# The first of a tile's six down units done in three split products instead of one float32 product

## What is computed

```python
x = x + conv_ref(ln_c(x))            # a mixer over 7 x 7 windows, then an MLP
t = to_tokens(x)
t = t + ffn_ref(ln_t(t))             # a gated feed-forward, 2 of 4 experts
# the part of conv_ref that the change touches (C = 96, HID = 384):
y = ln(xr, ln2_w, ln2_b)
y = gelu(y @ W1 + b1) @ W2 + b2
return xr + y
```

## Time and profile before

| | before |
|---|---|
| median of 3 runs | 1864.97 us (1864.04 to 1866.19) |
| the profiled execution | 1863.09 us, of which the profile's span is 1861.4 us |
| PE busy | 1809.9 us, 97% |
| DVE busy | 1527.7 us, 82% |
| ACT busy | 1489.4 us, 80% |
| POOL busy | 1432.4 us, 77% |

### The profile page before, as it was taken

The page is one execution under the profiler, slowest core; times in us unless marked ns, Lnnn a source line. Parts: engine busy times, 40 slices in busy tenths (PEclk is TensorE's granted clock), DMA queues, the critical chain, the costliest instruction groups (busy, mean ns, idle before and its releaser), DMA issues.

```text
span 1861.4 us, 35592 instructions
## 1 busy us (share of the span) xinstructions
PE 1809.9 (97%) x8486; PEld 1258.2 (68%) x8486; DVE 1527.7 (82%) x6498; ACT 1489.4 (80%) x2823; POOL 1432.4 (77%) x1097
## 2 busy tenths in 40 slices
PE   5999999999999999999998999999999999999997
PEld 3566665666656666556776777777777777777775
DVE  6899999999999999987886777777777777777775
ACT  1677777777777777778997999999999999999996
POOL 3388888888888888876886878887777777777776
PEclk9999999999999999999998999999999999999999
DMA  6253443344443334335667766666666666666662
GB/s 192 84 166 121 129 125 122 110 122 126 125 125 113 121 121 127 108 124 156 203 208 233 218 214 210 212 213 204 210 210 209 209 205 205 205 205 212 214 209 82
DMA packets 139737, 312.03 MB, mean 168 GB/s; under 512 B 35066, under 2 KB 43925, under 8 KB 139530
## 3 DMA queue, kind: packets, MB, share of 16 engines
q1 hardware_dynamic: 104424, 249.10, 44.5%
q0 software_dynamic: 32000, 58.87, 9.0%
q10 hardware_dynamic: 3106, 1.78, 0.5%
HBM read 243.43 MB, written 67.19 MB: 167 GB/s over the span
## 4 chain that ended last, share of the span: by engine, by line
PE 53%; POOL 23%; issue 13%; DVE 7%; ACT 0%; DVEq 0%; POOLq 0%; ACTq 0%
POOL sorted_rows L522 12%; PE mix_ps L1298 8%; PE mix_ps L1300 8%; PE mix_ps L1299 8%; POOL rstd_xt L511 6%; PE turn_ps L1284 4%; PE up_ps L1284 4%; POOL rstd_r L498 4%; PE turn_ps L1285 4%; PE up_ps L1285 4%; PE turn_ps L1286 4%; PE up_ps L1286 4%; PE tok_ps L1309 4%; PE y_ps L1221 2%; DVE rows L857 1%
## 5 line engine op out<-in xcount | busy, mean ns | idle before, releaser
L570 POOL DMA_INDIRECT out<-out_sb,idx x412 | 430.3, 1045 | 240.8 <-DVE out_sb L1077 127.3
L1036 DVE TENSOR_TENSOR g_lo<-g,g_hi 128x512 fp32r<-128x512 f32 x618 | 423.9, 687 | 194.8 <-ACT g_hi L698 194.4
L522 POOL DMA_INDIRECT sorted_rows<-rows,pos x392 | 452.3, 1154 | 116.7 <-issue 102.4
L698 ACT CAST g_hi<-g 128x512 fp32r<-128x512 f32 x618 | 381.5, 617 | 13.1
L546 POOL TENSOR_TENSOR ex<-euler,rows 128x16 f32<-128x16 f32 x103 | 306.3, 2974 | 0.4
L1173 PE MATMUL y_ps<-g,d_mlp 128*100 128x512 f32 x588 | 292.7, 592 | 0.2 <-ACT g L630 0.2
L1298 PE MATMUL mix_ps<-g_hi,ew 128*96 128x512 f32 x618 | 244.7, 396 | 0.2 <-DVE g_lo L1036 0.2
L1300 PE MATMUL mix_ps<-g_lo,ew 128*96 128x512 f32 x618 | 244.5, 396 | 0.0
L1299 PE MATMUL mix_ps<-g_hi,ew 128*96 128x512 f32 x618 | 243.6, 394 | 0.0
L630 ACT ACTIVATE g<-up_ps 128x512 f32<-128x512 f32 x294 | 170.7, 597 | 64.6 <-PE up_ps L1166 54.6
L692 ACT ACTIVATE g<-up_ps 128x512 f32<-128x512 f32 x308 | 183.7, 597 | 39.8 <-PE up_ps L1286 26.9
(11 more groups left out here) (185 smaller groups left out, 3964.5 us busy)
## 6 DMA issues: line engine op xcount, KB each, us to landing
ew<-expert_w SPq DMA_DIRECT2D x206, 384.0 KB, 4.1
ew<-expert_w SPq DMA_DIRECT2D x206, 288.5 KB, 3.6
rows<-sorted_rows SPq DMA_DIRECT2D x103, 394.0 KB
x_in<-in_x SPq DMA_DIRECT2D x49, 384.0 KB, 3.1
x_raw_t<-in_x_chan SPq DMA_DIRECT2D x49, 384.0 KB, 4.9
rstd_t<-rstd_rows SPq DMA_DIRECT2D x49, 384.0 KB, 4.0
out<-out_sb,idx POOLq DMA_INDIRECT x412
sorted_rows<-rows,pos POOLq DMA_INDIRECT x392
```

The lines of the kernel that those rows point to most:

```text
L522: pool.indirect_dma_start(out=sorted_rows[:, :], out_offset=bass.IndirectOffsetOnAxis(ap=pos[:, r, s:s + 1], axis=0), in_=rows[:, r, s, :] ...
L570: pool.indirect_dma_start(out=out_rows, out_offset=bass.IndirectOffsetOnAxis(ap=idx[:, r, s:s + 1], axis=0), in_=out_sb[:, r, s, :], in_of ...
L698: act.copy(g_hi[:, n % PART_RING, :], g[:, n % G_RING, :]).then_inc(hi_done, 1)
L1036: dve.tensor_tensor(g_lo[:, n % PART_RING, :], g[:, n % G_RING, :], f(g_hi[:, n % PART_RING, :]), ALU.subtract).then_inc(lo_done, 1)
```

## The change

Unit 0 of each tile (the first of six, in period p for tile p) is no longer multiplied in one float32 product. Its values are split: ScalarE casts the high part (`first_hi`, between `gelu` 0 and `gelu` 1) and VectorE subtracts it for the low part (`first_lo`, between `positions` and the statistics of the mixer output). TensorE then makes three products of the parts with `d0_hi` and `d0_lo`, the parts of the unit's weights, which VectorE makes once at the start. The other five units stay as they are.

```diff
+        d0_hi = sb("d0_hi", [P, CG], F32R)
+        d0_lo = sb("d0_lo", [P, CG], F32R)
...
+            def first_hi(t):
+                act.wait_ge(gelu_done, UNITS * t + 1)
+                if t >= 1:
+                    act.wait_ge(down_done, UNITS * (t - 1) + 1)
+                act.copy(g_hi[:, PART_RING - 1, :], g[:, UNITS * t % G_RING, :]).then_inc(first_hi_ok, 1)
...
                 if tile(p):
                     gelu(p, 0)
+                    first_hi(p)
                     gelu(p, 1)
...
+                dve.wait_ge(gate_sums, GATE_SUMS)
+                dve.tensor_copy(d0_hi[:, :], d_mlp[:, 0, :]).then_inc(first_down_parts, 1)
+                dve.wait_ge(first_down_parts, 1)
+                dve.tensor_tensor(d0_lo[:, :], d_mlp[:, 0, :], f(d0_hi[:, :]), ALU.subtract).then_inc(first_down_parts, 1)
...
+            def first_lo(t):
+                dve.wait_ge(first_hi_ok, t + 1)
+                dve.tensor_tensor(g_lo[:, PART_RING - 1, :], g[:, UNITS * t % G_RING, :], f(g_hi[:, PART_RING - 1, :]),
+                                  ALU.subtract).then_inc(first_lo_ok, 1)
...
                 if p == KNOWN + 2:
                     dve.wait_ge(base_set, KNOWN + 1)
                     list_blocks(0, 0)
+                if tile(p):
+                    first_lo(p)
                 if tile(r):
                     dve.wait_ge(xr_summed, r + 1)
...
                 if k == 0 and m >= 1:
                     pe.wait_ge(y_copied, m)
+                if u == 0:
+                    pe.wait_ge(first_down_parts, 2)
+                    pe.wait_ge(first_lo_ok, t + 1)
+                    pe.matmul(y_ps[0:CG, :], d0_hi[:, :], g_hi[:, PART_RING - 1, :], start=True, stop=False)
+                    pe.matmul(y_ps[0:CG, :], d0_lo[:, :], g_hi[:, PART_RING - 1, :], start=False, stop=False)
+                    pe.matmul(y_ps[0:CG, :], d0_hi[:, :], g_lo[:, PART_RING - 1, :], start=False, stop=False).then_inc(down_done, 1)
+                    return
```

More of the change, by code:

```diff
@@ L258, in build_program @@
         h_summed, xr_summed, xr_turned = (sem(n) for n in ("h_summed", "xr_summed", "xr_turned"))
+        first_down_parts, first_hi_ok, first_lo_ok = sem("first_down_parts"), sem("first_hi_ok"), sem("first_lo_ok")
         up_done, down_done, y_turned = sem("up_done"), sem("down_done"), sem("y_turned")
```

## The result

| | before | after |
|---|---|---|
| median | 1865.49 us (1864.04 to 1866.81, 5 runs) | 2011.17 us (2010.47 to 2012.46, 5 runs) |
| span of the profiled execution | 1861.4 us | 2008.9 us |
| mean granted TensorE clock over the span | 0.995 | 0.962 |

The changed kernel is slower: the ratio is 1.0782, 95% interval 1.0769 to 1.0796. That is 145.7 us more, where the prediction had 89.9 and its range ended at 1970.

The account below looks back on a forecast made before the run. TensorE, streaming without a gap, bounds the kernel; a new wait for VectorE's low part closes a loop of 18.51 us a tile against 16.56. Over all tiles 89.9 us more: 1864.97 + 89.9 = 1954.9 us, range 1938 to 1970.

Parts of the forecast that it names:

- What bounds, and the wait: TensorE streams at 16.56 us a tile; VectorE, only 0.5 us late, makes down 0 wait for the low part.
- The loop's length: Down 0 through `to_channels`, `y_hi`, `y_lo` and `first_lo` back to down 0: 18.51 us a tile, 1.95 more.
- The hand-over from VectorE's subtraction to the product: From the end of `first_lo` to TensorE's first split product: 0.15 us, bounds 0.05 and 0.25.
- TensorE's gain: Down 0 as three split products takes 0.70 us instead of 0.86 in float32, saving 0.155 us a tile.
- ScalarE's cast: `first_hi` between gelu 0 and 1 charged nothing; without cover from TensorE's wait, up to 1.0 us a tile.
- VectorE's own loop: VectorE's work per tile plus the subtraction, 16.56 + 0.69 = 17.25 us; as rival "VectorE alone grows" 1897 us, 6%.
- First and last tiles and the sum: Tile 4 late by 6.3 us, tiles 5 to 44 add 78.0, tile 45 3.6, tiles 46 to 48 2: 89.9.
- The clock falls: Rival, 4%: TensorE's 2 us gap per tile lowers its clock for 5 us, 2.5 us each in 45 tiles, 2067 us.
- The gap is far nearer to the first: TensorE's 2 us gap resembles a 1.79 us idle stretch that kept 2.4 GHz, not the 5.83 us one at 1.2.

Follow-up runs that it names:

- filled kernel: Changed kernel plus seven throwaway TensorE products per tile ahead of the wait for the low part; 1954.12 us, ratio 1.0482 to the kernel before.

## Why the prediction was wrong, point by point

- **What bounds, and the wait.** Right. TensorE streams before; VectorE can be moved up by half a microsecond and no more; the wait for the low part closes a loop through `to_channels`, `y_hi` and `y_lo`.
- **The loop's length.** 18.51 predicted, 18.44 in tiles with the full clock. The gap was put at 2.08 and is 1.89 to 1.91. `y_lo` waits as said, but 0.6 us and not some 1; in a tile with the full clock VectorE stands another 0.61 us ahead of `add_x2`, for `turn_y`. The hand-over from VectorE's subtraction to the product, taken as 0.15, is 402.24 - 402.09 = 0.15. The rest is small: `y_hi` to `y_lo` takes 0.03 instead of 0.05, `y_lo` to `first_lo` 7.17 (414.28 to 421.45) for 7.16, and down 0 to the end of `to_channels` 9.20 (422.28 to 431.48) for 9.26.
- **TensorE's gain.** 0.155 us a tile, measured 0.16.
- **ScalarE's cast.** Nothing predicted; measured ratio 1.0002 (0.9992 to 1.0011). The bound of 1.0 us a tile without cover was too careful.
- **VectorE's own loop**, used for a rival only: 17.25 predicted, 16.96 measured. The duration of 0.69 stood for a step of 0.60, and the wait for GpSimd was taken as fixed, but 0.2 us of it was slack.
- **First and last tiles and the sum.** 89.9 predicted; with the gap filled the kernel takes 89.6 us more than before. The forecast of 1954.9 us is the time of that kernel, 1954.1, with a filled gap, which had no part in it. That it is so near is in part luck, since the terms err both ways. In the filled kernel down 0 is 8.8 us later than before in tile 4 (predicted 6.3), and 81.5 in tile 44, so the 40 tiles add 72.7 (predicted 78.0); tile 45 adds 3.5 (3.6), and what is behind it 4.7 (2).
- **The step that failed** is in the rival *The clock falls*: "The gap is far nearer to the first", with 4%. It set one idle stretch of 1.79 us, after which the clock stayed up, against one of 5.83, after which it was down, and took the nearer. Two errors are in it. One stretch is one case, and at the same gap the clock falls in some tiles and not in others: at 1.89 us 9 of 40 tiles would have read like that row. And the gap comes in some 45 tiles, and whether it brings the clock down goes by where the tile lies in the order of the falls, so a chance for the whole kernel was the wrong form for it; it should have been a share of tiles, and with both ends of that share in the range. So the sum charged the clock nothing, where the runs show 57 us (2011.17 against 1954.12 with the gap filled). The price of the rival was also mis-sized, in the other direction: 2.5 us a tile in 45 tiles, 2067 us, where it is 1.61 in 34.

The Trainium skill (TensorE: Matmul & The Clock Gate, Part 1) says that what watches TensorE's activity runs free of the kernel, so that the point at which the clock changes varies with where the work lands. The runs agree: a gap that is the same in every tile brings the clock down in some tiles and not in others, 31, 29 or 9 of 40 by its length, and the place of the fall moves on from tile to tile (0.40, 0.85, 1.27 us behind down 0). What the prediction took from that page, that a gap as in rows 9 keeps the clock up, the measurements don't bear out: gaps of 1.33 to 1.89 us brought it down. The rule of the Trainium skill (TensorE: Matmul & The Clock Gate, Step-by-step: what each phase is for) that matmuls stay in program order was borne out: up 2 needs nothing from down 0, and in the timelines it stands behind it, 403.00 after 402.24.

## What to carry to other kernels

When a change gives a streaming TensorE a wait that comes once in each round of a loop, sum the loop as usual, and then charge the clock for each round by itself: a gap that left the clock up once may bring it down in most rounds. Where such a gap has to stay, products that feed nothing are a cheap cure and a sharp test; here seven of them a tile, 1.6 us of work, took 57 us off the changed kernel. They cure the clock alone: the 90 us of the loop stay. And before an operand for TensorE is put on another engine, look at where in that engine's order it would be made against where TensorE needs it: an engine with 18% of idle time still had only half a microsecond to give at that place.

None of the versions beats the kernel before. VectorE's 0.60 us a tile outweigh the 0.16 that TensorE gains, even where no wait of TensorE is in the way.

## What the runs showed of the hardware that I had not expected

Behind a gap of 1.89 us TensorE runs at its full clock for a while, 0.3 to 1.6 us in the steady tiles, and only then falls to 1.2 GHz, for 3.41 us, while it is busy without a break. A gap of 1.33 us did so in 9 of 40 tiles, one of 1.18 us in 1 of 40, one of 0.86 us in none. The tiles that fall come in a regular order, at 1.33 us each fourth, from tile 10 on. What exactly is counted, idle time alone or also the short products of `sum_xr` ahead of the gap, these runs don't tell apart: in all of them the gap ends at the start of down 0, and the fill changes both its length and what stands right ahead of it.
